# A decoder's gated-attention phase: the closing of each next batch's expert output is spread over three rounds, and the decay inputs move to later rounds

## The chip, the cores and the metric

One core of one Trainium2 chip runs the whole program. Times are microseconds of the device for one execution. The core has a matrix engine (TensorE, PE in the profile), a vector engine (VectorE, DVE), a scalar engine (ScalarE, ACT), GpSimd (POOL) and queues that issue transfers. They run their own instruction lists and meet only through semaphores. Lower is better.

## The reference, cut to what matters

The program is a decoder of two layers on `x` of shape (4, 512, 128): attention, cross attention and a mixture of experts, and then again gated linear attention, cross attention and a second mixture. After every block comes `x = layernorm(x + block(x))`. The change lies in the gated attention and in the end of the first mixture:

```python
q = silu(x @ Wq); k = silu(x @ Wk); v = x @ Wv      # 16 heads of 64
log_alpha = -softplus(x @ Wa + ba)
cum = cumsum(log_alpha, axis=1)
decay = exp(where(causal, cum[:, :, :, None] - cum[:, :, None, :], -inf))
o = ((q @ k.T) * decay) @ v
o = (o - mean) / sqrt(var + 1e-5) * gn_w + gn_b     # over sequence and head width
out = (o * sigmoid(x @ Wg)) @ Wo
...
# the mixture before it, whose result this phase starts from:
mixed = sum(topk_expert_outputs * topk_weights, axis=2)
x = layernorm(x + mixed)
```

## The kernel before, in words

The gated attention (`phase_d`) works on 4 batches of 8 head pairs. One pair is a **round**, g = 0 to 31 (four more empty the pipeline); b = g // 8 is the batch and s = g % 8 the place in it. Each engine has its own copy of the loop over g, and the order of the calls in it is written out by hand; an engine never takes a later instruction first.

In round g TensorE (lines 879 to 921) computes the state product of the pair before (`d_state(g - 1)`, L841), the query and key projections of the next pair (`d_proj(g + 1, 0)` and `(.., 1)`, L815 to L817, three matmuls each), the decays of the next pair (L796, L804, L806), the scores (L826), the gate projection of the pair before (`d_proj(g - 1, 2)`, again L815 to L817, after the second L806), a transpose (L832), and the output of pair g - 2 (`d_out`, L852 and L858). Then follows what only some rounds have: the group mean (`d_mean`, L868), a transpose of a closed batch (`turn_x`, L498), two value projections (`d_v`, L785), the alpha product (`d_alpha`, L759), the decay sums (`d_sums`, L767 to L771). A round is reckoned here from one first L841 to the next.

VectorE in round g: the state (`d_st`, L1762 and L1766), the two gated projections of the next pair (`d_silu`, L1728), the scores times decay (`d_at`, L1750), the decayed keys (`d_kd`, L1739), splits of weights and of x (L1494, L1495), statistics of pair g - 2 (`d_stats`, L1774 to L1780). After these comes what only some rounds have: `d_gated` (L1820, s = 1 and 5), `close_x`, `d_z` and `d_sp` (L1700 to L1708), `d_lsel` (L1369 to L1374 and a copy, L1715), `d_gate`. The next round begins with L1762 again.

`close_x(MOE[2], b)` ends the mixture of batch b: it waits for the gathered rows, adds them with their weights (8 instructions, L1674), takes statistics (L1307 to L1312), works out the reciprocal root in 11 small dependent instructions (L1317 to L1322) and writes the normalised x (L1332). Batch 0 is closed ahead of the phase, batches 1 to 3 inside the loop. Then `turn_x` and, on ScalarE, `keep_xT` (L959) lay the batch out transposed; `d_alpha`, `d_z`, ScalarE's `d_softplus` (L1175, L1176: an Exp and a Ln, each with a table load), `d_sp`, `d_sums`, `d_lsel` and ScalarE's `d_kdec` (L1182) follow on it. In rounds with s = 0 or 4 from g = 8 on, ScalarE also has `d_affine` (L1241), which in its list stands ahead of `d_softplus`.

Small products on TensorE share banks 6 and 7 in turn (`take_next`): each one waits until the reader of the product two places before it has read. So the gate projection of round g waits for VectorE's first L1728 of the same round, and a product that comes two places behind the decay sums waits for VectorE's `d_lsel`:

```python
            i = 6 + turn[0] % 2
            turn[0] += 1
            where[key] = bank[i]
            return take(pe, i, reader, value)
```

Of the kernel before, what the change touches and what calls it, by code (L numbers as in the profile page):

```python
# [35 lines left out]
NT = S // P  # L36
# [42 lines left out]
def decoder(nc, T):  # L79

    with ExitStack() as ctx:
# [13 lines left out]
        x_all = x_ext[:, :, 0:D]  # L95
        xT_all = sb("xT_all", [P, NB, S])
        yT = sb("yT", [P, S])
        res = sb("res", [P, NT, D])
# [136 lines left out]
        xh_D, xl_D = ([W0_low[:, 2048 + (2 * i + j) * S:2048 + (2 * i + j + 1) * S] for j in range(2)] for i in range(2))  # L235
        Q, K, V_, GATE = range(4)
        D_SPLITS = [(V_, 0), (Q, 0), (K, 0), (GATE, 0), (V_, 1), (Q, 1), (K, 1), (GATE, 1)]
        wqE, wkE, wvE, woE = (W0[:, i * 512:(i + 1) * 512] for i in range(4))

        ctxT = sb("ctxT", [P, NB * C])  # L240
# [223 lines left out]
        def _(pe):  # L464
# [405 lines left out]
            def phase_d():  # L870
                loaded(pe, "D", DMA_COUNT["D"])
                turn_x(PC)
                d_alpha(0)
                for t in range(NT):
                    d_v(0, 0, t)
                d_sums(0)
                d_proj(0, 0)
                d_proj(0, 1)
                d_decays(0)
                d_decay_to(0, 0)  # L880
                d_decay_to(0, 1)
                for g in range(32 + 4):
                    b, s = g // 8, g % 8
                    if 1 <= g <= 32:
                        d_state(g - 1)
                    if g + 1 < 32:
                        d_proj(g + 1, 0)
                        d_proj(g + 1, 1)
                        d_decays(g + 1)
                        d_decay_to(g + 1, 0)  # L890
                    if g < 32:
                        d_scores(g)
                    if g + 1 < 32:
                        d_decay_to(g + 1, 1)
                    if 1 <= g <= 32:
                        d_proj(g - 1, 2)
                    if g < 32:
                        d_kturn(g)
                    if 2 <= g < 34:
                        d_out(g - 2)  # L900
                    if s in (2, 6) and g >= 6:
                        d_mean((g - 6) // 4, 0)
                    if s in (3, 7) and g >= 7:
                        d_mean((g - 7) // 4, 1)
                    if g >= 16:
                        tail(PD + b - 2, s + 8)
                    if g in (1, 5, 9):
                        turn_x(PC + g // 4 + 1)
                    if g < 32:
                        if b:  # L910
                            tail(PD + b - 1, s)
                        if s in (2, 3):
                            d_v(b, 1, 2 * s - 4)
                            d_v(b, 1, 2 * s - 3)
                        if b + 1 < NB:
                            if s == 2:
                                d_alpha(b + 1)
                            if s == 4:
                                d_sums(b + 1)
                            if s in (6, 7):  # L920
                                d_v(b + 1, 0, 2 * s - 12)
                                d_v(b + 1, 0, 2 * s - 11)
# [9 lines left out]
        def _(act):  # L932
# [311 lines left out]
            def phase_d():  # L1244
# [9 lines left out]
                for g in range(32 + 4):  # L1254
# [10 lines left out]
                        d_affine((g - 8) // 4)  # L1265
                    if g >= 16:
                        tail(PD + b - 2, s + 8)
                    if g in (1, 5, 9):
                        keep_xT(PC + g // 4 + 1)
                    if g < 32:  # L1270
                        if b:
                            tail(PD + b - 1, s)
                        if s in (2, 3):
                            d_v(b, 1, 2 * s - 4)
                            d_v(b, 1, 2 * s - 3)
                        if b + 1 < NB:
                            if s == 2:
                                d_softplus(b + 1)
                            if s == 4:
                                d_kdec(b + 1)  # L1280
                            if s in (6, 7):
                                d_v(b + 1, 0, 2 * s - 12)
                                d_v(b + 1, 0, 2 * s - 11)
# [10 lines left out]
        def _(dve):  # L1294
# [370 lines left out]

            def close_x(m_, b):

                x = x_all[:, 4 * b:4 * b + 4, :]
                w = per_pair(wk, m_, b)
                dve.wait_ge(x_ready, m_["w0"] + b)  # L1670
                dve.wait_ge(sem(f"M_g{b}"), 32 + 16 * (m_["b0"] // NB))
                for k in range(m_["k"]):
# [5 lines left out]
                        dve.wait_ge(sem("M_cb"), m_["b0"] + b + 1)  # L1678
                    else:
                        link(i)  # L1680
                ln_stats(res)
                ln_apply(res, x).then_inc(x_ready, 1)


            def d_split_x(b):
# [137 lines left out]
            def phase_d():  # L1823
# [12 lines left out]
                for g in range(32 + 4):  # L1836
# [6 lines left out]
                    if g < 32:  # L1843
                        d_at(g)
                        d_kd(g)
                    for i in range(3 + 2 * g, min(5 + 2 * g, len(D_SPLITS))):
                        d_split_w(i)
                    if s == 5 and b + 1 < NB:
                        d_split_x(b + 1)
# [7 lines left out]
                        d_gated((g - 9) // 4, (0, 1, 2, 3))  # L1857
                    if g >= 16:
                        tail(PD + b - 2, s + 8)
                    if g in (0, 4, 8):  # L1860
                        close_x(MOE[2], g // 4 + 1)
                    if g < 32:
                        if b:
                            tail(PD + b - 1, s)
                        if b + 1 < NB:
                            if s == 2:
                                d_z(b + 1)
                                d_sp(b + 1)
                            if s == 4:
                                d_lsel(b + 1)  # L1870
                    if s in (3, 7) and g >= 7:
                        d_gate((g - 7) // 4)
# [190 lines left out]
```

## Time and profile before

| what | us |
|---|---|
| median of 3 runs | 1574.44 (1573.21 to 1575.3) |
| the profiled execution, its own time | 1578.1 |
| its span, first to last instruction | 1576.3 |
| TensorE matmuls busy | 1282.9 (81%) |
| VectorE busy | 849.2 (54%) |
| ScalarE busy | 834.8 (53%) |
| mean granted clock of TensorE | 0.921 of full |

The rows further down begin with the start and the duration in microseconds; a bracket at the end of a row is the time for which the engine stood idle before it, and what ended that. The granted clock is given in parts of 2.4 GHz; 0.5 is 1.2 GHz.

### The profile page before, as it was taken

To read this page: it belongs to the slowest core of one execution; us is meant where nothing else is said; L and a number is where in the kernel's file an instruction comes from. 1 tells how busy PE (TensorE), PEld (TensorE's weight loads), DVE (VectorE), ACT (ScalarE), POOL (GpSimd) and SP (SyncE) were. 2 spreads that over 40 slices of the span, in tenths; PEclk is the share of its full clock that TensorE was granted. 3 is DMA by queue.
4 is the path that set the end of the run, shared out by engine and by line. 5 is a ranking of instruction groups with operands and counts; after the bars stand their busy time and mean duration, and the time that the engine had idled before them with its cause. 6 is when DMAs were issued, how large, how long until landed. Compare 5 with 4: busy or idle time off the path is not lost.

```text
span 1576.3 us, 22676 instructions
## 1 busy us (share of the span) xinstructions
PE 1282.9 (81%) x6903; PEld 739.8 (47%) x6934; DVE 849.2 (54%) x2752; ACT 834.8 (53%) x1893; POOL 503.2 (32%) x473
## 2 busy tenths in 40 slices
PE   5999999999999987987645957788888886787552
PEld 2434444444344335544425955556565664444341
DVE  3544453364444336367552347777677876557535
ACT  4777677677767734544313634456465662344121
POOL 2555455445545512132453521001011010122242
PEclk9999999999999998998777979899999997898676
DMA  7235223220000000000026821000000000000053
GB/s 211 55 78 86 55 55 55 55 78 1 1 1 1 1 1 0 1 1 1 14 94 180 246 88 41 1 1 1 1 1 1 1 1 8 20 1 4 17 151 104
DMA packets 77701, 67.56 MB, mean 43 GB/s; under 512 B 5040, under 2 KB 68656, under 8 KB 77328
## 3 DMA queue, kind: packets, MB, share of 16 engines
q1 hardware_dynamic: 73488, 57.69, 15.2%
q0 software_dynamic: 3520, 7.27, 1.3%
q8 instruction: 60, 0.98, 0.3%
q10 hardware_dynamic: 576, 1.16, 0.2%
q14 instruction: 57, 0.47, 0.1%
HBM read 37.69 MB, written 28.41 MB: 42 GB/s over the span
## 4 chain that ended last, share of the span: by engine, by line
PE 63%; DVE 19%; issue 7%; ACT 6%; POOL 2%; DMA 2%; SPq 1%; DVEq 0%; POOLq 0%; ACTq 0%
PE bank L550 8%; PE bank L532 7%; PE bank L540 6%; PE bank L479 6%; PE bank L655 3%; PE bank L522 3%; PE bank L612 3%; PE bank L626 3%; PE bank L720 3%; PE bank L728 2%; PE bank L858 2%; DVE work L1381 2%; PE bank L641 2%; PE bank L852 1%; ACT work L996 1%
## 5 line engine op out<-in xcount | busy, mean ns | idle before, releaser
L1909 POOL TENSOR_TENSOR work<-work 128x512 f32<-128x512 f32 x256 | 266.1, 1040 | 272.5 <-DVE work L1389 272.5
L996 ACT ACTIVATE work<-bank,work 128x512 f32<-128x512 f32 x256 | 176.5, 689 | 117.4 <-DVE work L1381 117.3
L1381 DVE TENSOR_REDUCE work<-bank 128x1 f32<-128x512 f32 x256 | 176.4, 689 | 77.3 <-PE bank L532 77.0
L540 PEld LDWEIGHTS bank<-cst,work 128*128 128x128 f32 x1024 | 110.5, 140 | 164.4 <-issue 103.6
L540 PE MATMUL bank<-cst,work 128*128 128x128 f32 x1024 | 160.0, 283 | 6.6 <-ACT work L1004 6.0
L1389 DVE RECIPROCAL work<-work 128x1 f32<-128x1 f32 x256 | 41.9, 164 | 223.4 <-ACT work L996 223.0
L1004 ACT ACTIVATE work<-bank 128x512 f32<-128x512 f32 x256 | 152.6, 596 | 0.5 <-PE bank L540 0.5
L1991 POOL TENSOR_TENSOR work<-work 128x512 f32<-128x512 f32 x32 | 40.8, 1274 | 335.0 <-PE bank L858 294.3
L532 PE MATMUL bank<-work 64*128 64x512 f32 x512 | 144.5, 641 | 3.4 <-ACT work L996 3.4
L550 PE MATMUL bank<-work 128*64 128x512 f32 x512 | 137.4, 617 | 0.7 <-ACT work L1004 0.7
L1949 POOL TENSOR_TENSOR work<-work 128x1232 f32<-128x1232 f32 (+1 forms) x32 | 55.5, 1733 | 247.8 <-DVE work L1462 247.8
L1444 DVE TENSOR_REDUCE work<-bank 128x6 f32<-128x462 f32 (+1 forms) x80 | 38.9, 535 | 108.9 <-PE bank L626 108.9
L479 PE MATMUL bank<-OT,W 128*128 128x512 f32 x208 | 95.7, 604 | 0.7 <-DVE am L1568 0.7
L532 PEld LDWEIGHTS bank<-work 64*128 64x128 f32 x512 | 38.7, 184 | 97.0 <-issue 60.5
L1977 POOL DMA_INDIRECT yt<-work x62 | 59.3, 957 | 77.4 <-DVE work L1631 75.0
L1160 ACT ACTIVATE work<-bank,W 128x128 f32<-128x128 f32 x166 | 48.4, 369 | 63.0 <-PE bank L720 63.0
L1107 ACT ACTIVATE work<-bank 128x512 f32<-128x512 f32 x96 | 53.0, 595 | 54.0 <-PE bank L641 54.0
L641 PE MATMUL bank<-cst,work 128*128 128x128 f32 x384 | 59.2, 305 | 26.7 <-POOL work L1949 19.3
L815 PE MATMUL bank<-W_low 128*128 128x512 f32 x96 | 47.0, 490 | 38.3 <-DVE work L1728 17.2
L1208 ACT ACTIVATE work<-bank,work 128x128 f32<-128x128 f32 x256 | 72.4, 384 | 10.5 <-PE bank L806 10.5
L522 PE MATMUL bank<-W 128*128 128x512 f32 x128 | 69.2, 626 | 6.2 <-ACT work L984 3.8
L626 PE MATMUL bank<-work 128*128 128x154 f32 x384 | 61.2, 312 | 14.6 <-DVE work L1449 14.6
(246 smaller groups left out, 2457.2 us busy)
## 6 DMA issues: line engine op xcount, KB each, us to landing
xs<-gat SPq DMA_DIRECT2D x18, 1040.0 KB, 12.0
W<-in_w SPq DMA_DIRECT2D x30, 322.0 KB, 3.4
W<-in_w SPq DMA_DIRECT2D x23, 193.0 KB, 2.5
work<-xs SPq DMA_DIRECT2D x62, 65.0 KB, 3.5
gat<-yt SPq DMA_DIRECT2D x12, 256.0 KB, 3.0
work<-in_w SPq DMA_DIRECT2D x9, 322.0 KB, 3.4
W<-in_v SPq DMA_DIRECT2D x1, 2048.0 KB, 11.4
x_ext<-in_x SPq DMA_DIRECT2D x4, 256.0 KB, 8.4
```

What stands on the lines that cost most here:

```text
L479: m = mm(where["y", w][:, :], out_w(ph)[:, p * P:(p + 1) * P], o_slot(w, p), start=(p == 0), stop=(p == n - 1))
L522: mm(out[:, :], w[:, p * P:(p + 1) * P], xnT[b % 2], start=True, stop=True).then_inc(sem(ready), 1)
L532: m = mm(out[hh][:, :], qA[g % 2][HALF[hh], t * P:(t + 1) * P], kA[g % 2][HALF[hh], :], start=True, stop=True)
L540: m = nc.tensor.transpose(out[:, k * P:(k + 1) * P], pA[u % 5][:, k * P:(k + 1) * P], ident)
L550: m = mm(bank[5][hh * DH:(hh + 1) * DH, :], v3(vA[p // 4], NT)[:, k, (2 * (p % 4) + hh) * DH:(2 * (p % 4) + hh + 1) * DH], v3(ptA[(2 * g + ...
L626: m = mm(out[:, (p % 3) * 2 * C:(p % 3 + 1) * 2 * C], v3(qTB, NPAIR)[:, p, t * P:(t + 1) * P], kd, start=True, stop=True)
L641: m = nc.tensor.transpose(out[:, i * P:(i + 1) * P], pB[u % 3][:, h * C:h * C + P], ident)
L996: A(pA[u % 5], bank[u % 3][:, :], ACT.Exp, bias=nmax[:, u % 8:u % 8 + 1], accum_out=rsum[0][:, u % 8:u % 8 + 1]).then_inc(sem("a_e"), 1)
L1004: A(v3(ptA[h % 4], NT)[:, :, t * P:(t + 1) * P], v3(bank[3 + u % 2][:, :], NT), ACT.Copy)\
L1208: i = A(dmD[g % 2][:, (NT * hh + c) * P:(NT * hh + c + 1) * P], bank[1 - hh][:, c * P:(c + 1) * P], ACT.Exp, scale=-1.0, bias=lcD[b % 2][: ...
L1381: V.tensor_reduce(nmax[:, u % 8:u % 8 + 1], bank[u % 3][:, :], AX, ALU.max, negate=True)\
L1909: G.tensor_tensor(pA[u % 5], pA[u % 5], rsum[1][:, u % 8:u % 8 + 1].to_broadcast([P, S]), ALU.mult)\
```

## The change

1. `close_x` of batches 1 to 3 is cut into `close_step` parts 0, 1 and 2 (sum; statistics and root; normalise), one in each of the rounds g = 4k, 4k + 1 and 4k + 2. It stood whole in the rounds 0, 4 and 8. Batch 0 is still closed whole.
2. `turn_x` and `keep_xT` of these batches move from rounds 1, 5 and 9 to 3, 7 and 11.
3. `d_alpha`, `d_softplus`, `d_z` and `d_sp` of the next batch move from s = 2 to s = 4, `d_sums`, `d_kdec` and `d_lsel` from s = 4 to s = 5, in batches 0, 1 and 2.
4. The weight splits 3 to 7 stand in rounds 0, 1, 2, 2 and 3 in place of 0, 0, 1, 1 and 2.
5. At the start of the phase TensorE's `d_sums(0)` stands after two of the four value projections, not after all four.

```diff
+        SPLITS_AT = {0: (3,), 1: (4,), 2: (5, 6), 3: (7,)}
...
-                for t in range(NT):
+                for t in (0, 1):
                     d_v(0, 0, t)
                 d_sums(0)
+                for t in (2, 3):
+                    d_v(0, 0, t)
                 d_proj(0, 0)
...
-                    if g in (1, 5, 9):
+                    if g in (3, 7, 11):
                         turn_x(PC + g // 4 + 1)
...
-                            if s == 2:
+                            if s == 4:
                                 d_alpha(b + 1)
-                            if s == 4:
+                            if s == 5:
                                 d_sums(b + 1)
...
+            def close_step(m_, b, part):
+
+                if part == 0:
+                    close_sum(m_, b)
+                elif part == 1:
+                    ln_stats(res)
+                    ln_rstd()
+                elif part == 2:
+                    ln_apply(res, x_all[:, 4 * b:4 * b + 4, :], rstd=False).then_inc(x_ready, 1)
...
-                    for i in range(3 + 2 * g, min(5 + 2 * g, len(D_SPLITS))):
+                    for i in SPLITS_AT.get(g, ()):
                         d_split_w(i)
...
-                    if g in (0, 4, 8):
-                        close_x(MOE[2], g // 4 + 1)
+                    if g < 12:
+                        close_step(MOE[2], g // 4 + 1, g % 4)
```

ScalarE's and VectorE's loops have the same changes of s and of g as TensorE's.

**The closing of batch 1, on VectorE.** Before, rounds 0 and 1 meet here: `d_kd`, two splits, the whole closing (its first rows).

```order
L1739 TENSOR_TENSOR work<-bank,work 128x512
L1494 CAST W_low<-W 128x512
L1495 TENSOR_TENSOR W_low<-W,W_low 128x512
L1494 CAST W_low<-W 128x512
L1495 TENSOR_TENSOR W_low<-W,W_low 128x512
L1674 SCALAR_TENSOR_TENSOR res<-gat,wk,x_ext 128x128 x4
L1674 SCALAR_TENSOR_TENSOR res<-gat,wk,res 128x128 x4
L1307 BN_STATS bn<-res 128x6 x4
```

After, the same place, where the lines have moved down by 3 or 17 to 19 (L1739 is L1756, L1494 is L1497, L1674 is L1693, L1307 is L1310):

```order
L1756 TENSOR_TENSOR work<-bank,work 128x512
L1497 CAST W_low<-W 128x512
L1498 TENSOR_TENSOR W_low<-W,W_low 128x512
L1693 SCALAR_TENSOR_TENSOR res<-gat,wk,x_ext 128x128 x4
L1693 SCALAR_TENSOR_TENSOR res<-gat,wk,res 128x128 x4
L1779 TENSOR_SCALAR work<-bank 64x3x64 x2
L1783 SCALAR_TENSOR_TENSOR work<-work 64x64 x4
L1745 SCALAR_TENSOR_TENSOR work<-work,bank 128x512 x2
L1767 SCALAR_TENSOR_TENSOR work<-bank,work 128x512 x2
L1756 TENSOR_TENSOR work<-bank,work 128x512
L1497 CAST W_low<-W 128x512
L1498 TENSOR_TENSOR W_low<-W,W_low 128x512
```

The statistics now stand behind the VectorE work of one more pair and one split.

**The alpha of batch 3, on VectorE at the ends of rounds 20 and 21.** Before, from the splits of x in round 21 (the decay sums were read in round 20):

```order
L1739 TENSOR_TENSOR work<-bank,work 128x512
L1494 CAST W0_low<-xT_all 128x512
L1495 TENSOR_TENSOR W0_low<-xT_all,W0_low 128x512
L1774 BN_STATS work<-bank 128x6
L1776 BN_AGGR work<-work 128x2
L1779 COPY work<-work 128x1
L1780 COPY work<-work 128x1
L1820 SCALAR_TENSOR_TENSOR OT<-work,OT 128x512 x4
L1762 TENSOR_SCALAR work<-bank 64x3x64 x2
```

After, the same place (L1837 is the L1820 of before, L1372 to L1377 and L1732 are `d_lsel`):

```order
L1791 BN_STATS work<-bank 128x6
L1793 BN_AGGR work<-work 128x2
L1796 COPY work<-work 128x1
L1797 COPY work<-work 128x1
L1837 SCALAR_TENSOR_TENSOR OT<-work,OT 128x512 x4
L1372 CAST work<-bank 16x512
L1373 TENSOR_TENSOR work<-bank,work 16x512
L1375 CAST work<-work 16x512
L1376 COPY work<-work 16x512
L1377 TENSOR_TENSOR work<-work 16x512
L1732 COPY work<-bank 128x128
L1779 TENSOR_SCALAR work<-bank 64x3x64 x2
```

`d_lsel` now stands in the same round as `d_gated` and the split of x, behind both.

**The softplus of batch 3, on ScalarE at the end of round 20.** Before, round 20 has the affine and `d_kdec`:

```order
L1223 ACTIVATE work<-bank 128x512
L1232 ACTIVATE OT<-bank 128x512
L1241 ACTIVATE OT<-OT,work 128x512 x4
L1182 ACTIVATE work<-work 128x64
L1218 ACTIVATE work<-bank 128x512 x2
L1198 ACTIVATE work<-bank 128x512
```

After (L1244 is the affine, L1178 and L1179 the softplus with its table load, L1221 the next tanh with its own):

```order
L1226 ACTIVATE work<-bank 128x512
L1235 ACTIVATE OT<-bank 128x512
L1244 ACTIVATE OT<-OT,work 128x512 x4
L1178 ACTIVATE work<-work 128x64
L1179 ACT_TABLE_LOAD
L1179 ACTIVATE work<-work 128x64
L1221 ACT_TABLE_LOAD
L1221 ACTIVATE work<-bank 128x512 x2
```

The softplus and its two table loads now stand behind the affine and ahead of the next pair's tanh.

## Rows read from the trace of the kernel before

**Rows 1.** The page: busy time and share of the span.

```profile
PE 1282.9 (81%) x6903; PEld 739.8 (47%) x6934; DVE 849.2 (54%) x2752; ACT 834.8 (53%) x1893; POOL 503.2 (32%) x473
```

**Rows 2.** Waits of TensorE, 935 to 1335 us: total, times, longest.

```profile
PE bank L815 <- DVE work L1728: 17.2, 9, 7.0
```

**Rows 3.** Timeline of TensorE at the closings of batches 2 and 3.

```profile
1012.10 0.77 PE L815 MATMUL bank<-W_low 128*128 128x512 f32 x1 [7.57 <-DVE work L1370]
...
1061.68 0.76 PE L815 MATMUL bank<-W_low 128*128 128x512 f32 x1 [4.78 <-DVE work L1728]
...
1066.93 0.66 PE L498 MATMUL bank<-cst,x_ext 128*128 128x128 f32 x4
...
1091.68 0.83 PE L841 MATMUL bank<-work 128*128 128x128 f32 x6
```

**Rows 4.** Stretches: busy us of PE, PEld, DVE, ACT, POOL; granted clock; DMA.

```profile
1060.00:1066.00 6.00, 4.32 (x19) 3.72 (x21) 3.94 (x8) 0.00 (x0) 0.00 (x0) 0.50 0.00 0
1106.00:1114.00 8.00, 6.73 (x61) 5.11 (x57) 7.53 (x16) 3.73 (x12) 1.28 (x1) 1.00 0.00 0
```

**Rows 5.** Timeline of VectorE, the closing of batch 3 in round 8.

```profile
1051.79 1.15 DVE L1674 SCALAR_TENSOR_TENSOR res<-gat,wk,x_ext 128x128 f32<-128x128 f32 x4
...
1054.14 0.87 DVE L1307 BATCH_NORM_STATS2 bn<-res 128x6 f32<-128x128 f32 x4
...
1057.85 1.12 DVE L1332 TENSOR_SCALAR x_ext<-res,mv,lnv 128x128 f32<-128x128 f32 x4
1058.88 0.71 DVE L1762 TENSOR_SCALAR work<-bank 64x192 f32<-64x192 f32 x2
```

**Rows 6.** Timelines at the phase's start: TensorE, VectorE, ScalarE.

```profile
942.78 0.77 PE L785 MATMUL bank<-W_low 128*128 128x512 f32 x1
...
948.84 0.29 DVE L1715 COPY work<-bank 128x128 f32<-128x128 f32 x1
...
945.44 1.28 ACT L1182 ACT_TABLE_LOAD   x1
```

**Rows 7.** Timeline of TensorE, rounds 19 to 23.

```profile
1172.50 0.91 PE L841 MATMUL bank<-work 128*128 128x128 f32 x6
...
1178.20 0.39 PE L804 MATMUL bank<-work,sel 128*128 128x512 bf16 x1 [1.43 <-ACT work L1198]
...
1191.56 1.05 PE L767 MATMUL bank<-cst,work 128*16 128x128 f32 x8
...
1193.04 0.89 PE L841 MATMUL bank<-work 128*128 128x128 f32 x6
1194.42 0.47 PE L815 MATMUL bank<-W_low 128*128 128x512 f32 x1 [0.50 <-DVE work L1370]
...
1196.21 0.47 PE L815 MATMUL bank<-W_low 128*128 128x512 f32 x1 [0.85 <-DVE work L1715]
...
1199.28 0.58 PE L815 MATMUL bank<-W_low 128*128 128x512 f32 x1
...
1202.39 0.94 PE L841 MATMUL bank<-work 128*128 128x128 f32 x6
...
1209.00 0.47 PE L815 MATMUL bank<-W_low 128*128 128x512 f32 x1 [0.26 <-DVE work L1728]
...
1212.00 0.39 PE L868 MATMUL bank<-work,cst 128*128 128x4 f32 x2
...
1221.47 0.83 PE L841 MATMUL bank<-work 128*128 128x128 f32 x6
```

**Rows 8.** Timelines of ScalarE and VectorE, rounds 18, 20 and 21.

```profile
1173.43 0.26 ACT L1175 ACTIVATE work<-work 128x64 f32<-128x64 f32 x1 [0.94 <-DVE work L1703]
...
1192.95 2.92 ACT L1241 ACTIVATE OT<-OT,work 128x512 f32<-128x512 f32 x4
...
1175.43 0.72 DVE L1762 TENSOR_SCALAR work<-bank 64x192 f32<-64x192 f32 x2
...
1203.59 2.69 DVE L1820 SCALAR_TENSOR_TENSOR OT<-work,OT 128x512 f32<-128x512 f32 x4
```

More of the change, by code:

```diff
@@ L1267, in phase_d @@
                         tail(PD + b - 2, s + 8)
-                    if g in (1, 5, 9):
+                    if g in (3, 7, 11):
                         keep_xT(PC + g // 4 + 1)
@@ L1276, in phase_d @@
                         if b + 1 < NB:
-                            if s == 2:
+                            if s == 4:
                                 d_softplus(b + 1)
-                            if s == 4:
+                            if s == 5:
                                 d_kdec(b + 1)
@@ L1666, in close_x, with close_sum @@
             def close_x(m_, b):
+                close_sum(m_, b)
+                ln_stats(res)
+                ln_apply(res, x_all[:, 4 * b:4 * b + 4, :]).then_inc(x_ready, 1)
+            def close_step(m_, b, part):
+                if part == 0:
+                    close_sum(m_, b)
+                elif part == 1:
+                    ln_stats(res)
+                    ln_rstd()
+                elif part == 2:
+                    ln_apply(res, x_all[:, 4 * b:4 * b + 4, :], rstd=False).then_inc(x_ready, 1)
+            def close_sum(m_, b):
                 x = x_all[:, 4 * b:4 * b + 4, :]
@@ L1680, in close_x @@
                         link(i)
-                ln_stats(res)
-                ln_apply(res, x).then_inc(x_ready, 1)
             def d_split_x(b):
@@ L1865, in phase_d @@
                         if b + 1 < NB:
-                            if s == 2:
+                            if s == 4:
                                 d_z(b + 1)
                                 d_sp(b + 1)
-                            if s == 4:
+                            if s == 5:
                                 d_lsel(b + 1)
```

## The prediction

> **What bounds the kernel now.** The page first: matmuls are busy 81% of the span, VectorE and ScalarE just over half [rows 1]. So TensorE sets the time wherever nobody keeps it waiting, and an edit that issues the same instructions in another order is worth what it takes from, or adds to, TensorE's waits. The waits of TensorE over the phase come next: the largest group is the projection L815 waiting for VectorE's L1728, 17.2 us in 9 waits, the longest 7.0 [rows 2]. The timeline says where. After the closing of batch 2 the first projection waited 7.57 us, after that of batch 3 the gate projection 4.78 [rows 3]; the 7.0 of [rows 2] is the closing of batch 1. The closing is one block on VectorE: 2.35 us of sum, 3.71 of statistics and root, 1.03 of normalising, 7.09 together (1051.79 to 1058.88) [rows 5]. VectorE cannot start the next pair's L1762 before it, and the gate projection starts 2.80 us after that L1762 (1058.88 to 1061.68) [rows 3, 5].
>
> A long wait costs twice. In 1060 to 1066 the granted clock is 0.50, the lower of its two levels, and it is 1.00 in 1106 to 1114, a stretch with short waits only [rows 4]. From gate projection to the end of the output product took 5.25 us at the low level (1061.68 to 1066.93) and 3.00 at full (1209.00 to 1212.00) [rows 3, 7]: 2.25 us for each wait after which the clock is down. What TensorE did before it fell was nothing, for 4.8 to 7.6 us.
>
> The Trainium skill, "TensorE: Matmul & The Clock Gate", section "HAM oscillation — how this bites in real kernels", takes the penalty as half of the time spent at the low level. For the six microseconds of [rows 4] that is 3.0 where the rows give 2.25; six falls would cost 18 by the page and 13.5 by the rows.
>
> **Where the change gains: rounds 0 to 11.** I followed the rounds one by one with the durations of before. VectorE's own chain from one L1762 to the next is some 7.2 us in a round with nothing extra, TensorE's 7.5; of extra work at the round's end about 1.8 us is free. The three closings cost TensorE 7.0, 7.57 and 4.78 us of idle time, another 1.5 us where ScalarE was late in the third, and three stretches of low clock, some 6.8 together: 27.7. The alpha of batches 1 and 2 in rounds 2 and 10 cost some 5 more (1.4 each at L804, as in 1178.20 [rows 7], and waits for banks). All of it goes, about 32.
>
> What comes in its place, at full clock, with the parts of [rows 5]:
> - Start: `d_sums(0)` can start at 942.78, when bank 6 is read, some 2.1 us earlier than it did. But it takes both banks, and the third and fourth value projections then wait for `d_lsel` and its copy (L1715). So the fourth ends 0.7 us after the copy, ScalarE reads it, and only then comes the table load, 1.28 us, that before ran at 945.44 under cover of `d_lsel` [rows 6]. The copy is 1.7 us earlier (948.84 to 947.1), the tanh behind it 1.0 later, the next exponential 0.6. Cost +0.6; the bounds are -1.9 (all of the earlier sums) and +1.3 (the whole load).
> - Round 0 ends with a split and the sum, 3.4 us: stall 1.5. Round 1 with a split and the statistics, 4.8: stall 3.0. Round 2 with two splits ahead of the statistics of the pair, which ScalarE's reads wait for: 1.4.
> - Round 4: sum 2.35, then `d_z`, softplus, `d_sp`: stall 4.2 in round 5, in two pieces, since the second projection also waits for `d_z`.
> - Round 5: split of x, statistics 3.71, then `d_lsel` with its 2.9 to the copy, all before round 6: 4.35 us idle, one projection, 1.0 more.
> - Round 8: sum; ScalarE's affine hides most: 0.3. Round 9: `d_gated` 2.6 and statistics 3.71 meet: 1.5 for a bank and 4.4 in one piece. The third parts, in rounds 2, 6 and 10, are 1.03 us and hidden by the value projections (1.4) behind the output product.
>
> Together some 22. Counted from round start to round start, round 12 begins at 1080.5 at full clock and 1091.68 before [rows 3]: **-11.2 us**, of which 0.8 is alpha not yet done.
>
> **Where it loses: rounds 12 to 15 and 19 to 23.** Nothing is closed here; only the alpha has moved, next to other work. Batch 3, by [rows 7, 8]:
> - Round 19 starts 0.8 earlier (no alpha), 1171.7, and has no wait of 1.43. Rounds 19 and 20 took 20.54 us (1172.50 to 1193.04); less the 1.5 of waiting, less 1.48 of sums (1191.56 to 1193.04), plus 0.8 of alpha: round 21 starts at 1190.1, and the output product ahead of it ends at 1189.3.
> - ScalarE starts the affine 1.39 us after that end (1191.56 to 1192.95) and is free 2.8 later: 1193.5. Then softplus, first Exp to the next L1762, 2.00 (1173.43 to 1175.43): 1195.5. L804 comes 2.77 after (1175.43 to 1178.20), at 1198.3, the gate projection 0.25 later. TensorE is through with its scores 4.3 us into a round (1178.20 less 1.43, from 1172.50), at 1194.4. **A new wait of 3.9 us.** Before, the affine stood over `d_lsel`, both hidden from each other; now VectorE waits for the Ln behind it.
> - The output product ends at 1201.5, the sums at 1203.0. VectorE has statistics 1.1, `d_gated` 2.6 (L1820), `d_lsel` to the copy 2.9, 0.4 to the projection: 1208.8 for the second, 1207.0 for the first (they are 1.79 apart at 1194.42 and 1196.21). **A new wait of 3.2 and then 1.1 us**, for 0.50 and 0.85 before.
> - Then as before: 3.07 to the gate projection (1196.21 to 1199.28), 12.47 to round 23 (1209.00 to 1221.47): it starts at 1224.3, for 1221.47. **+2.8 us.**
>
> Batch 2 has the same in rounds 12 to 15, but the 2.3 us that its round 10 gained is already in the -11.2: **+4.9**. At full clock the change so gives -11.2 + 4.9 + 2.8 = **-3.5 us**.
>
> **The clock.** The new waits are 3.0 (round 2), 2.5 (5), 4.35 and 1.0 (6), 4.4 (10), 3.9 (13), 3.2 and 1.1 (14), 3.9 (21), 3.2 and 1.1 (22). Before, three long waits lowered the clock in this phase and none of the short ones, up to 1.58 us, did. A wait of 3.9 lies between, nearer to the 4.78 that did; I count all of 3.9 us and more as falls (4 of them), the pair 3.2 + 1.1 as falls too, since they are one projection apart (2), and half for each of rounds 2 and 5 at about 2 us. With 2.25 us each this is 6 x 2.25 + 1.5 = 15, less some 1.3 where VectorE is last anyway: **+13.7**. Bounds: nothing, and 8 x 2.25 = 18.
>
> **Sum.** -3.5 + 13.7 = +10.2. The walk is made on the profiled execution (1578.1, 1576.3 of it span; 3.7 above the median), which would go to about 1588. On the median: 1574.4 + 10 = **1584 us**. Every long wait that the closing left is cut, and the number of waits long enough to lower the clock goes from three to some six.
>
> **Rivals.**
> 1. *The clock holds.* New waits of 3 to 4.4 us are shorter than any of the three that lowered it here. Then the time is 1574.4 - 3.5 = **1571**. Against: 3.9 to 4.4 is only a little under 4.78. Chance 0.15. It decides the sign: with two falls (4.5 us) the change is already no gain.
> 2. *The spreading works as it reads.* VectorE is idle almost half of the span [rows 1] and might take parts of 2.35, 3.71 and 1.03 us in its gaps, with the alpha as cheap as before. Then the 27.7 us of the closings go and the new waits stay at some 10: about **1560**. What speaks against it is that only 1.8 us per round is free and that in rounds 5 and 9 two pieces meet. Chance 0.07.
> 3. *Some falls only.* Only two or three of the six waits lower the clock, or they are shorter than worked out: +1 to +4, **1577**. Chance 0.20.
> 4. *My sum*, six or more falls: 1578 to 1591, **1584**, chance 0.58.
>
> **How the numbers follow.** What a measurement of this kernel can tell from no change is about 0.2%, 3.1 us: the three runs of before span 2.1. Faster by more than that is rival 2 and half of rival 1 with a little of 3: 0.17. Within it: the other half of 1, most of 3 and the edge of 4: 0.19. Slower 0.64. The range reaches from the full-clock case, 1570, to all eight falls with the start at its bound, 1591; less than 2 in 10 is outside, rival 2 above all. The likeliest case alone has 1578 to 1591.
>
> **What would show each step.** After the change, no wait of TensorE over 5 us in the phase; at the start, the tanh behind `d_kdec` about 1 us later, ScalarE's table load after the fourth value read. In rounds 13 and 21 a wait of L804 for ScalarE's L1198 (L805 and L1201 then) of about 4 us, with VectorE waiting some 4 us for the Ln; in rounds 14 and 22 a wait of the first projection for `d_lsel`, 3 us, and one of 1 behind it. Stretches at 0.50 after these, six in place of three. If the stretch of rounds 12 to 23 is not longer than before, my softplus step is wrong; if it is longer by under 8 us, the clock was oversized. If the first twelve rounds gain less than 5 us, the closings' parts cost more than I took.

## The result and the profile after

| | before | after |
|---|---|---|
| median | 1573.83 us, 4 runs (1573.15 to 1575.3) | 1586.56 us, 4 runs (1584.61 to 1587.15) |
| ratio to before | | 1.0077 (95% interval 1.006 to 1.0095) |
| profiled execution, its own time and span | 1578.1, 1576.3 | 1587.15, 1585.3 |
| mean granted clock | 0.921 | 0.916 |

The change makes the kernel 0.8% slower. The page of after has the same work as [rows 1], with 4.9 us more of matmul time on the same 6903 matmuls:

```profile
PE 1287.8 (81%) x6903; PEld 744.9 (47%) x6934; DVE 850.7 (54%) x2752; ACT 835.3 (53%) x1893; POOL 503.4 (32%) x473
```

**Where the time went.** The rounds of both traces were laid beside each other by their first state product, counted from the start of the phase (its L498 or L499; 935.52 in the span of before, 933.17 in that of after). The difference, after less before, in us:

| start of round | 1 | 2 | 6 | 7 | 10 | 12 | 14 | 15 | 18 | 21 | 22 | 23 | 26 | 32 |
|---|---|---|---|---|---|---|---|---|---|---|---|---|---|---|
| later by | 1.6 | -5.1 | -7.7 | -0.9 | -7.6 | -4.0 | 2.3 | 3.4 | 3.4 | 0.4 | 8.2 | 8.6 | 10.1 | 10.2 |

The phase starts 2.35 earlier in its span and what follows it takes 1.2 longer, so the span grows by 9.0. Nothing of the edit stands ahead of the phase, and in the eleven traces of this document it starts anywhere from 930.5 to 935.7, so the 2.35 is no merit of the change. The medians differ by 12.7, more than the spans, because the traced execution of before was 4.3 above its kernel's median and that of after 0.6 above. From one trace to another a step of the table over the same instructions repeats within some 0.1 us where the clock does the same in both, and moves by about 1.6 with a short fall of it. The table is read by its steps. The closings gain in rounds 1, 5 and 9, as meant. Much of it is lost at once, 6.8 in round 6 and 4.5 in round 10. From round 12 on nothing is gained that lasts: from round 12 to 15 it loses 7.4 us, from 18 to 23 5.2 and from 25 to 26 1.6, together 14.2.

The waits of TensorE over the phase (total, times, longest) show what took the place of [rows 2]. The largest group is no longer for VectorE's projections but for ScalarE:

```profile
PE bank L805 <- ACT work L1201: 16.7, 8, 3.8
PE bank L816 <- DVE work L1745: 11.2, 9, 4.0
PE bank L816 <- DVE work L1373: 6.3, 3, 4.1
PE bank L816 <- ACT work L1226: 5.7, 4, 1.6
...
PE bank L771 <- ACT work L1226: 3.5, 2, 1.8
```

On TensorE's timeline the place of [rows 7] now has these waits in two rounds (L842 is the state product, L805 the decays, L771 the second decay-sum product, L816 the projections):

```profile
1191.13 0.91 PE L842 MATMUL bank<-work 128*128 128x128 f32 x6
...
1199.18 0.61 PE L805 MATMUL bank<-work,sel 128*128 128x512 bf16 x1 [3.78 <-ACT work L1201]
...
1207.71 0.43 PE L771 MATMUL bank<-work,cst 128*128 128x64 f32 x2 [1.76 <-ACT work L1226]
1208.20 0.89 PE L842 MATMUL bank<-work 128*128 128x128 f32 x6
1210.23 0.47 PE L816 MATMUL bank<-W_low 128*128 128x512 f32 x1 [1.14 <-DVE work L1373]
...
1212.01 0.47 PE L816 MATMUL bank<-W_low 128*128 128x512 f32 x1 [0.85 <-DVE work L1732]
```

The first wait is explained by ScalarE's timeline of the same stretch. The affine ends at 1194.5, and only then come the Exp, the Ln and the tanh of the next pair (L1221). There are two table loads of 1.28 us, one ahead of the Ln and one ahead of the tanh; the Exp has none of its own, in before neither (it starts at 1173.43, the Ln's load at 1173.70), although the description of the kernel before gives it one. L805 waits for L1201 behind that tanh:

```profile
1191.61 2.92 ACT L1244 ACTIVATE OT<-OT,work 128x512 f32<-128x512 f32 x4
1194.43 0.24 ACT L1178 ACTIVATE work<-work 128x64 f32<-128x64 f32 x1
1194.69 1.28 ACT L1179 ACT_TABLE_LOAD   x1
1195.98 0.26 ACT L1179 ACTIVATE work<-work 128x64 f32<-128x64 f32 x1
1196.26 1.28 ACT L1221 ACT_TABLE_LOAD   x1
...
1198.52 0.60 ACT L1201 ACTIVATE work<-bank 128x512 f32<-128x512 f32 x1
...
1207.06 0.60 ACT L1226 ACTIVATE work<-bank 128x512 f32<-128x512 f32 x1 [5.67 <-DVE OT L1837]
```

VectorE stands 4.03 us for that Ln with the whole next pair behind it, and later runs `d_gated` (L1837) and `d_lsel` (L1372 to L1732) in one piece:

```profile
1196.27 0.23 DVE L1725 SCALAR_TENSOR_TENSOR work<-work 128x64 f32<-128x64 f32 x1 [4.03 <-ACT work L1179]
...
1206.10 2.67 DVE L1837 SCALAR_TENSOR_TENSOR OT<-work,OT 128x512 f32<-128x512 f32 x4
1208.69 0.67 DVE L1372 CAST work<-bank 16x512 bf16<-16x512 f32 x1
```

The closings' parts are felt most in rounds 5, 6 and 10, where they meet the softplus, `d_lsel` or `d_gated`:

```profile
1006.24 0.61 PE L805 MATMUL bank<-work,sel 128*128 128x512 bf16 x1 [2.24 <-ACT work L1201]
...
1017.66 0.77 PE L816 MATMUL bank<-W_low 128*128 128x512 f32 x1 [4.07 <-DVE work L1373]
...
1067.79 0.76 PE L816 MATMUL bank<-W_low 128*128 128x512 f32 x1 [3.96 <-DVE work L1745]
```

And the clock. Of these stretches of after (length; busy us of PE, PEld, DVE, ACT, POOL; granted clock; DMA) each holds one fall, in the start and in rounds 2, 5, 6, 10, 13, 14, 21 and 25; before has three falls among its rounds (1, 5 and 9), the last of them in [rows 4]:

```profile
943.00:947.00 4.00, 2.64 (x7) 1.94 (x8) 2.03 (x5) 0.65 (x2) 0.00 (x0) 0.73 0.00 0
964.00:968.00 4.00, 2.98 (x12) 2.55 (x11) 3.79 (x16) 0.37 (x1) 0.01 (x1) 0.66 0.53 178
1004.00:1008.00 4.00, 1.76 (x6) 1.20 (x6) 3.80 (x9) 3.89 (x11) 0.00 (x0) 0.78 0.01 2
...
1018.00:1022.00 4.00, 3.50 (x9) 1.55 (x9) 3.81 (x11) 1.64 (x4) 0.00 (x0) 0.50 0.02 4
...
1069.00:1073.00 4.00, 4.00 (x31) 3.46 (x30) 1.66 (x3) 0.60 (x1) 0.39 (x1) 0.73 0.00 0
...
1102.00:1106.00 4.00, 4.00 (x19) 3.25 (x19) 2.49 (x5) 1.89 (x7) 0.00 (x0) 0.59 0.00 0
1111.00:1116.00 5.00, 3.59 (x8) 1.90 (x10) 4.71 (x13) 1.22 (x3) 0.00 (x0) 0.66 0.00 0
1199.00:1203.00 4.00, 3.82 (x14) 3.06 (x14) 2.49 (x6) 2.29 (x9) 0.00 (x0) 0.50 0.00 0
1254.00:1257.00 3.00, 2.31 (x11) 2.16 (x12) 2.78 (x5) 1.10 (x5) 0.00 (x0) 0.74 0.00 0
```

A value between 0.5 and 1 says that the low level held for a part of the stretch. There are nine falls in place of three, seven of them shorter than that of [rows 4]. Round 22 has the waits of round 14 and no fall:

```profile
1205.00:1225.00 20.00, 16.09 (x92) 9.90 (x93) 13.30 (x33) 5.57 (x15) 2.53 (x2) 1.00 0.00 1
```

### The profile page after: what moved, and what is told of

It is laid out like the page before. It is cut to its first block, busy times and chain, and to the rows that moved or that the text cites. A ratio compares the mean times of both kernels' runs of the same rounds, so it can differ in the third digit from the quotient of the medians.

```text
span 1585.3 us, 22679 instructions
## 1 busy us (share of the span) xinstructions
PE 1287.8 (81%) x6903; PEld 744.9 (47%) x6934; DVE 850.7 (54%) x2752; ACT 835.3 (53%) x1893; POOL 503.4 (32%) x473
## 4 chain that ended last, share of the span: by engine, by line
PE 62%; DVE 19%; issue 7%; ACT 7%; POOL 2%; SPq 1%; DMA 1%; POOLq 0%; DVEq 0%; ACTq 0%
PE bank L551 8%; PE bank L533 7%; PE bank L541 6%; PE bank L480 6%; PE bank L656 3%; PE bank L523 3%; PE bank L613 3%; PE bank L721 3%; PE bank L627 3%; PE bank L729 2%; PE bank L859 2%; DVE work L1384 2%; PE bank L642 2%; PE bank L853 1%; ACT work L999 1%
## 5 line engine op out<-in xcount | busy, mean ns | idle before, releaser
L1211 ACT ACTIVATE work<-bank,work 128x128 f32<-128x128 f32 x256 | 72.7, 382 | 10.2 <-PE bank L807 9.6
L816 PE MATMUL bank<-W_low 128*128 128x512 f32 x96 | 49.2, 513 | 28.1 <-DVE work L1745 11.2
## 6 DMA issues: line engine op xcount, KB each, us to landing
xs<-gat SPq DMA_DIRECT2D x18, 1040.0 KB, 11.8
```

What stands on the lines that cost most here:

```text
L1211: i = A(dmD[g % 2][:, (NT * hh + c) * P:(NT * hh + c + 1) * P], bank[1 - hh][:, c * P:(c + 1) * P], ACT.Exp, scale=-1.0, bias=lcD[b % 2][: ...
```

## The experiments

Theory A, that of the prediction: the closings' parts gain a few us, the moved alpha loses more, a good part of it through the clock. Its rival B: the parts themselves are the loss, and where the alpha stands hardly matters. A second question is how the loss divides into ScalarE's collision (round 13 and 21), VectorE's (14 and 22) and the clock. The ratios are to before in the same set of runs, with 95% intervals. Times in the phase are counted from its start, as in the table above.

### 1. The alpha of batches 2 and 3 back in its old rounds

The changed kernel, with the rounds of the alpha and its sums as before from batch 1's on; the alpha of batch 1 stays where the change put it, since batch 1 is closed later. The same edit stands in ScalarE's and VectorE's loops.

```diff
-                            if s == 4:
+                            if s == (4 if b == 0 else 2):
                                 d_alpha(b + 1)
-                            if s == 5:
+                            if s == (5 if b == 0 else 4):
                                 d_sums(b + 1)
```

> The changed kernel, but for batches 2 and 3 (decided in rounds 8 and up) alpha and softplus are back at s = 2 and the decay sums back at s = 4; the first batch's stay at 4 and 5, since its x is closed later. My theory (the loss is made in rounds 12 to 15 and 19 to 23, where softplus stands behind the affine and the decay sums behind the gated product): both losses go, about 7 and 5 us, and round 10 gets some 3 us of stall back: 1575 us, with the same start of round 6 as in the changed kernel. Rival (the three parts of the closing are the loss): within 3 us of the changed kernel's 1586.6.

Measured: 1575.1 us, ratio 0.9997 (0.9985 to 1.0008). Round 12 starts 3.8 earlier than before, round 15 still 3.9 earlier, and 2.3 remain at the end, after a fall of the clock in round 17 (1.6). Against the trace of after that is 10.2 + 2.3 = 12.5 us, and the ratios say the same (0.9997 for 1.0077, 12.6 us). So the whole loss belongs to the alpha of batches 2 and 3, and B falls. Whether the closings in parts with the new start gain anything is not shown: 2.3 us between two single traces, but a ratio whose interval holds 1. With the start's 1.0012 (experiment 3) taken off, the parts alone would gain some 2.4 us, which is an estimate; no run has them alone.

### 2. The alpha alone

The kernel before, with `d_alpha` and its followers moved as in the change in the batches 1 and 2 (b > 0), and nothing else.

```diff
-                            if s == 2:
+                            if s == (2 if b == 0 else 4):
                                 d_alpha(b + 1)
-                            if s == 4:
+                            if s == (4 if b == 0 else 5):
                                 d_sums(b + 1)
```

> The kernel before, with alpha and softplus of batches 2 and 3 alone moved to s = 4 and the sums to s = 5; closings whole, start as before. My theory: 5 us lost per batch, 1573.8 + 10 = 1584 us, with waits of TensorE for ScalarE of 3.8 us in rounds 13 and 21. Rival (alpha is free to move): 1574 us.

Measured: 1590.89 us, ratio 1.0089 (1.0076 to 1.0102), 14 us over before where 10 were expected. Its waits show the same collision without any part of a closing:

```profile
PE bank L804 <- ACT work L1198: 15.6, 8, 3.8
```

From the start of round 12 to that of 15 it loses 6.8 us, from 21 to 23 8.0, and in rounds 17 and 25 1.6 each, where the clock fell. Less what rounds 10 and 11 (2.4) and 18 to 20 (2.9) gain, the two batches cost 4.4 and 5.1, as counted. What had not been counted are the 3.2 of falls in rounds that the edit doesn't touch.

### 3. The start alone

The kernel before, with `d_sums(0)` after two of the four value projections (the last piece of the change's diff).

> The kernel before with only the first decay sums moved between the second and the third value projection. My theory: both banks are taken, the table load is uncovered, and the clock may fall: +0.6 to +1.6 us, 1575 us. Rival (sums that are ready earlier help): -1.9 us, 1572 us.

Measured: 1578.89 us, ratio 1.0012 (1.0003 to 1.0021). Round 1 starts 1.63 later and all later ones by the same. The start costs 1.6 us in the traces, 1.9 by the ratio, and is not paid back.

### 4. The first new wait filled

The changed kernel, with 16 idle products in rounds 13 and 21, where TensorE waits for ScalarE. Their result is never read and the real work is the same. If the low clock comes from TensorE's doing nothing, it must stay away.

```diff
                         d_scores(g)
+                    if g in (13, 21):
+                        pe.wait_ge(sem("d_o"), g - 2)
+                        for _ in range(16):
+                            mm(bank[5][:, :], ident_b[:, :], mask[:, :], start=True, stop=True)
```

> The changed kernel, with 16 idle products of constants (128x512, bf16, into a bank that is overwritten next) behind the scores of rounds 13 and 21, which keep TensorE at work during the waits of 3.8 us. The result is unchanged. My theory (each fall of the clock costs about 2.25 us): the stretches at 0.50 behind these two waits go and the time falls by 3 to 4.5 us, to about 1583. Rival (VectorE and ScalarE are last there, so TensorE's clock costs nothing): 1586.6 us, unchanged.

Measured: 1589.08 us, ratio 1.0077 (1.0064 to 1.009): no gain over the change. The stretches say why:

```profile
1098.00:1106.00 8.00, 7.75 (x58) 4.86 (x59) 5.49 (x14) 7.08 (x16) 0.00 (x0) 1.00 0.00 0
1112.00:1116.00 4.00, 3.64 (x8) 1.73 (x10) 3.78 (x12) 1.47 (x4) 0.00 (x0) 0.50 0.00 0
1196.00:1205.00 9.00, 8.65 (x67) 5.44 (x68) 6.25 (x15) 7.33 (x17) 0.00 (x0) 1.00 0.00 0
1210.00:1214.00 4.00, 3.76 (x8) 1.82 (x10) 3.77 (x11) 1.23 (x3) 0.00 (x0) 0.50 0.00 0
```

Where the fillers ran, the clock stayed at full, and round 14 starts level with before in place of 2.3 later. One round on, the waits for the sums' readers brought the clock down instead, and by round 23 the kernel is 8.3 later than before, against 8.6 in after. Part of this is a fall in round 17 (0.57 in 1158 to 1162), which cost 1.6 and which after does not have. My expectation overlooked that the second waits suffice by themselves, in round 22 too, where after had kept the full clock.

### 5. Both new waits filled

The same, with 8 idle products ahead of the second decay-sum product of batches 2 and 3 and 5 behind the state product of rounds 14 and 22.

```diff
                 m.then_inc(sem("d_LT"), 1)
+                if b >= 2:
+                    pe.wait_ge(sem("d_dm"), 16 * b - 2)
+                    for _ in range(8):
+                        mm(bank[0][:, :], ident_b[:, :], mask[:, :], start=True, stop=True)
                 out = take_next(pe, ("d_lc", b), sem("d_lcs"), b + 1)
...
                         d_state(g - 1)
+                    if g in (14, 22):
+                        for _ in range(5):
+                            mm(bank[0][:, :], ident_b[:, :], mask[:, :], start=True, stop=True)
```

> As the run with 16 idle products in rounds 13 and 21, and besides 8 such products ahead of the second decay-sum product of these rounds and 5 behind the state product of rounds 14 and 22, so that TensorE works through most of both waits. The result is unchanged. My theory (in the run before, the falls only moved from the first wait to the second): with both covered no stretch at 0.50 stays in rounds 13, 14, 21 and 22, and each batch gains 2 to 4 us over the changed kernel: 1581 us on the scale of 1586.6. Rival (the clock costs nothing there, others are last): 1586.6.

Measured: 1579.96 us, ratio 1.0027 (1.0015 to 1.0039), for 1.0077 of the change. The clock stays at full through both places:

```profile
1098.00:1106.00 8.00, 7.60 (x55) 4.84 (x54) 7.74 (x17) 4.49 (x13) 1.26 (x1) 1.00 0.00 0
1190.00:1215.00 25.00, 23.70 (x159) 14.61 (x158) 19.42 (x47) 12.13 (x30) 2.53 (x2) 1.00 0.00 1
```

With the clock up, rounds 12 to 15 lose 5.1 us and rounds 18 to 23 2.8, and no round after them anything. In after the same stretches lose 7.4 and 5.2, and round 25 1.6. So of after's 14.2 us behind round 12 the clock makes 6.3 and the collisions make 7.9. This division rests on one trace of each kernel, this one the fastest of twelve executions (1577.3), and whatever the fillers themselves cost is in the 7.9. Another 2.0 us by which this kernel is ahead at round 12 are no merit of the fillers: ahead of them the instructions are those of after. Most of it is round 5, where the same wait of 2.24 us was followed by a fall in after (0.78 in 1004 to 1008, above) and by none here:

```profile
1004.00:1008.00 4.00, 2.47 (x17) 2.03 (x19) 3.83 (x9) 4.00 (x12) 0.00 (x0) 1.00 0.00 2
```

### 6. The softplus ahead of the affine

The changed kernel, with ScalarE's `d_softplus` called before `d_affine` in rounds with s = 4. Then the two swap who waits, if VectorE's `d_sp` is the one that keeps the next pair.

```diff
+                    if s == 4 and b + 1 < NB:
+                        d_softplus(b + 1)
                     if s in (0, 4) and g >= 8:
                         d_affine((g - 8) // 4)
...
-                            if s == 4:
-                                d_softplus(b + 1)
```

> The changed kernel with ScalarE's softplus ahead of the affine in rounds with s = 4. Theory A (what ends TensorE's wait of 3.8 us is ScalarE's whole list, affine and softplus and table loads, whatever their order): no gain, 1586 to 1589 us, the wait of TensorE for L1201's counterpart at 3.8 us or a little more. Theory B (VectorE waiting for the Ln is what counts): the Ln comes 2.2 us earlier, twice, 1582 us.

Measured: 1588.54 us, ratio 1.0081 (1.0067 to 1.0095), as the change. The wait of the decays even grew, from 3.78:

```profile
1199.60 0.61 PE L805 MATMUL bank<-work,sel 128*128 128x512 bf16 x1 [4.48 <-ACT work L1201]
```

In its trace the phase takes 3.7 longer than in after; it has falls in rounds 17 and 22 that after does not have (and none at the start or in 25), and the ratios do not tell the two kernels apart. So putting the softplus first gains nothing; my reading, which no run separates further, is that both stand between two pairs, and the decays wait for the tanh behind both.

### 7. The sums alone

The kernel before, with only `d_sums`, `d_kdec` and `d_lsel` of batches 2 and 3 at s = 5. The alpha and the softplus stay at s = 2, so ScalarE's collision in rounds 13 and 21 can't arise.

```diff
-                            if s == 4:
+                            if s == (4 if b == 0 else 5):
                                 d_sums(b + 1)
```

> The kernel before, with only the decay sums (and what reads them) of batches 2 and 3 moved from s = 4 to s = 5; alpha and softplus stay at s = 2, closings whole. If the collision with the gated product is the larger part of what alpha_only lost (14 us over before): 1573.8 + 8 to 10, about 1583. If it is the affine and softplus: 1573.8 + 2 to 4, about 1577. I take the second to be likelier by my sum (waits of 3.2 and 1.1 us in place of 1.4 and 1.5, with one fall of the clock per batch).

Measured: 1585.87 us, ratio 1.0059 (1.0046 to 1.0073), against some 1577 expected. The step that I had thought the lesser half makes most of the loss: 9.3 us of 14.0 by the ratios, 9.8 of 11.8 in the phase of the two traces. The alpha and the softplus add the rest, 4.7 or 1.9; it is little for waits of 3.8, since moving them also ends the waits that they caused in their old rounds. Rounds 13 and 14 cost 4.4 us and 21 and 22 4.9, and falls of the clock in rounds 17 and 25 2.9 and 1.6. These last 4.5, in rounds that the edit doesn't touch, are the larger part of what the expectation missed; experiment 2 has 3.2 of the same. TensorE's timeline in round 21 shows what I had not counted:

```profile
1207.04 0.43 PE L770 MATMUL bank<-work,cst 128*128 128x64 f32 x2 [1.76 <-ACT work L1223]
...
1209.56 0.77 PE L815 MATMUL bank<-W_low 128*128 128x512 f32 x1 [0.55 <-DVE work L1370]
1211.35 0.77 PE L815 MATMUL bank<-W_low 128*128 128x512 f32 x1 [0.17 <-DVE work L1715]
```

The second decay-sum product takes the bank of the gate projection. Its reader is ScalarE's tanh of the gate, L1223, and that one waits for VectorE's `d_gated`, which reads what it will overwrite (5.67 us in after, at 1207.06 above). At s = 4 there is no `d_gated`; at s = 5 the sums stand behind it.

### 8. Batch 3 closed whole in round 14

From the change: the alpha as in experiment 1, the start as before, batches 1 and 2 closed in thirds, and batch 3 closed whole at the end of round 14, whose end on TensorE is long (before it takes 19 us). Its `turn_x` and `keep_xT` move to round 15.

```diff
-                    if g < 12:
+                    if g < 8:
                         close_step(MOE[2], g // 4 + 1, g % 4)
+                    if g == 14:
+                        close_x(MOE[2], 3)
...
-                    if g in (3, 7, 11):
-                        turn_x(PC + g // 4 + 1)
+                    if g in (3, 7, 15):
+                        turn_x(PC + (1, 2, 0, 3)[g // 4])
```

> A version of my own: closings of batches 1 and 2 in thirds, alpha of batches 2 and 3 at s = 2 and sums at s = 4, start as before, and batch 3 closed whole in round 14, where VectorE waits 8.27 us for TensorE's output projection, with its transpose in round 15. Theory: the start's 1.6 us and the third closing's 4 to 5 us go, against the run with alpha back (0.9997 of before): ratio about 0.9955, 1567 us. Rival (a closing costs its 7 us wherever VectorE has it): ratio 0.999 or more.

Measured: 1568.51 us, ratio 0.9947 (0.9934 to 0.996). Rounds 9 and 10 take 22.0 us for 29.7 before. Round 14 takes 19.1, as before: VectorE has done with the whole closing and still waits for TensorE:

```profile
1113.64 1.14 DVE L1691 SCALAR_TENSOR_TENSOR res<-gat,wk,x_ext 128x128 f32<-128x128 f32 x4
...
1119.70 1.12 DVE L1333 TENSOR_SCALAR x_ext<-res,mv,lnv 128x128 f32<-128x128 f32 x4
1121.99 0.72 DVE L1777 TENSOR_SCALAR work<-bank 64x192 f32<-64x192 f32 x2 [1.17 <-PE bank L842]
```

The rounds 5, 6 and 7, though, take 42.6 us for 39.2 before (40.6 in experiment 1): closing batch 2 in thirds in rounds 4 to 6, with batch 1's alpha in rounds 4 and 5, costs more there than closing it whole had. Some 2 of these 3.4 us are one fall of the clock in round 5, which experiment 1 does not have with the same instructions and the same wait (2.25 and 2.24). First experiment 1, then this kernel:

```profile
1008.00:1012.00 4.00, 3.67 (x34) 3.03 (x35) 3.87 (x8) 2.82 (x10) 0.05 (x1) 1.00 0.00 0
1008.00:1012.00 4.00, 3.69 (x15) 3.04 (x15) 3.09 (x7) 2.80 (x10) 0.00 (x0) 0.63 0.00 0
```

### 9. Batch 2's parts in rounds 6, 8 and 9 as well

```diff
-                    if g < 8:
-                        close_step(MOE[2], g // 4 + 1, g % 4)
+                    if g < 4:
+                        close_step(MOE[2], 1, g)
+                    if g in (6, 8, 9):
+                        close_step(MOE[2], 2, (6, 8, 9).index(g))
```

The turn of batch 2 moves to round 10.

> The version with batch 3 closed in round 14, and batch 2's three parts moved from rounds 4, 5 and 6 to rounds 6, 8 and 9, with its transpose in round 10: away from the softplus of round 4 and the decay sums of round 5, into rounds where VectorE's time is short or ScalarE's affine makes TensorE wait anyway. Theory (a part costs only where it meets other work behind the same output product): rounds 5 to 8, 42.6 us in the run with batch 3 in round 14, fall to 32 to 34, and round 9 loses about 1: 8 us less, 0.9947 goes to about 0.990, 1560 us. Rival (the parts cost their time in any round): within 2 us of 1568.5.

Measured: 1565.04 us, ratio 0.9926 (0.9913 to 0.9939): faster than both kernels, 0.3% short of what was expected. Rounds 5 to 7 take 32.5 us. Rounds 9 and 10 take 27.3 for 22.0 in experiment 8, where I had expected 1 us more: the statistics stand where batch 2's alpha is, and TensorE waits five times, each time briefly. The clock also fell there (0.57 in 1046 to 1050).

```profile
1044.27 0.39 PE L805 MATMUL bank<-work,sel 128*128 128x512 bf16 x1 [1.54 <-ACT work L1199]
1046.27 0.47 PE L816 MATMUL bank<-W_low 128*128 128x512 f32 x1 [1.40 <-DVE work L1743]
...
1053.75 0.47 PE L816 MATMUL bank<-W_low 128*128 128x512 f32 x1 [1.28 <-ACT work L1224]
...
1058.48 0.47 PE L816 MATMUL bank<-W_low 128*128 128x512 f32 x1 [1.28 <-DVE work L1743]
...
1063.10 0.47 PE L786 MATMUL bank<-W_low 128*128 128x512 f32 x1 [0.75 <-DVE work L1805]
```

## Why the prediction was right, and where its terms were off

The forecast was 1584 us, slower, at a chance of 0.64; 1586.56 came, inside the likeliest case's 1578 to 1591. Inside the phase the trace of after is 10.2 us longer, for +10.2 in the sum. That the sum fits so closely is partly luck, as its terms show, and the medians differ by 12.7 rather than 10.2.

- **The closings' gain, rounds 0 to 11.** -11.2 at full clock and three falls' worth of clock (6.8) made -4.5 at round 12; -4.0 came. Experiment 5, with one fall less, has -6.0. Experiment 1 ends 2.3 us ahead of before in its trace, but its ratio of 0.9997 does not show that anything of it lasts. The waits came nearly as worked out: for a stall of 1.5 behind round 0, 1.19; for 3.0 behind round 1, 1.01 and 2.54 in experiment 5 (1.01 and 0.96 in after, where the clock had fallen ahead of the second); for 4.2 in round 5, 1.51 and 2.24; for 4.35 and 4.4 in rounds 6 and 10, 4.07 and 3.96. My test for this step, a gain of under 5 us by round 12 as a sign that the parts cost more than I took, was badly put: it was met by the 4.0, but my own sum had -4.5 there with the clock.
- **The start.** +0.6 was forecast, 1.6 came (experiment 3 too). The mechanism is as told: the fourth value is read, and only then comes the table load, at 947.56. In experiment 4, which has the same start, the clock did not fall there (1.00 in 945 to 949 for 0.73 in 943 to 947 of after), and round 1 came 0.77 later than before. Experiment 6, with no fall there either, has 0.48; experiments 1, 3 and 5, with one, have 1.6 to 1.7. The term missing was the clock: the waits of 0.99 and 0.85 after a stretch of little work were not counted as such that may lower it.
- **The softplus, rounds 13 and 21.** A wait of 3.9 of L804 for ScalarE was forecast, 3.81 and 3.78 came, with VectorE 4.03 behind the Ln for "some 4".
- **The sums, rounds 14 and 22.** A wait of 3.2 and one of 1.1 were forecast. The trace has 1.76, 1.14 and 0.85 (0.17 in round 14): nearly the same total, in other pieces. The step "`d_sums` costs 1.48 and then the projection waits for `d_lsel`" left out that the second product itself waits for the gate's tanh behind `d_gated`. Experiment 7 shows it alone.
- **Rounds 12 to 15 and 18 to 23 at full clock.** +4.9 and +2.8 were forecast; with the clock kept up (experiment 5) they are +5.1 and +2.8. This is the best part of the prediction, though the terms listed for VectorE in round 21 (1.1, 2.6, 2.9 and 0.4 from 1201.5) end at 1208.5 and not at 1208.8, which would give +2.5.
- **No wait over 5 us** held for the rounds: the longest is 4.07. The one of 5.6 for ScalarE's L1235, at the phase's end, is in before too.
- **The clock.** 2.25 us per fall was too much for these. The pairs of rounds 13 and 14 and of 21 and 22 were counted as four falls; three came (13, 14 and 21), and they cost 4.7 together, 1.6 each. A short fall in round 17 or 25 costs 1.6 too, and the longer one of experiment 7 in round 17 2.9, so the price goes with the length, and most of these are shorter than that of [rows 4]. From round 12 to 23 the kernel loses 12.6 where the terms give some 15. The whole wait was also taken for what lowers the clock. In before it was down well before the waits ended: 0.84 in 1059 to 1060, while the wait of 4.78 ran from 1056.90 to 1061.68. So a wait of 3.9 was not clearly short of those that lowered it. (The sum has a slip as well: half of each of rounds 2 and 5 at about 2 us makes 2.0, and 1.5 was added.) On the other side there are more falls: nine in place of the six to seven counted. One of them, in round 25, follows waits of 1.52 and 0.99, which the trace of before has as well, at 1.00 throughout. Too few falls at too high a price made about the right sum for the whole phase.
- **The rivals.** The clock did not hold (1), the alpha was not as cheap as before (2), and there were more falls, not fewer (3). With the fillers of experiment 5 the full-clock case can be seen: 1.0027, and not the 0.998 that rival 1 gave, since falls in the first rounds remain and fillers have to be issued.

What stays open is why a wait of a given length is followed by a fall in one kernel and not in another. The wait of 2.24 in round 5 did it in after and not in experiment 5. The pair of 1.5 and 1.0 stands in rounds 17 and 25 of all eleven traces, and the clock fell there in 11 of the 22 cases. The Trainium skill, "TensorE: Matmul & The Clock Gate", section "What's actually happening", says that the window in which TensorE's activity is watched runs freely and does not start with the kernel, so that the cold start of one and the same kernel differs from run to run. The two traces of round 5 are in keeping with that (0.78 and 1.00), but no run here shows the window itself, and no kernel was traced twice. It was not tried to shift such a wait by small steps.

## What to carry to other kernels

A block that is moved to a later round must be read against everything that stands in the new round, on every engine: here the softplus met ScalarE's affine (a wait of 3.8), and the decay sum, which cost more on balance, took a bank whose reader waits for VectorE's long `d_gated`. Cutting a block into thirds gained little where the parts met other work (experiment 1, 0.9997, of it 0.0012 the cost of the start), and more where they were moved away from it (experiment 9, 0.9926 for 0.9947); one place where the engine that sets the time has a long stretch of its own (round 14) hid the whole 7 us block at no cost. And a wait on TensorE has to be priced twice, itself and the clock behind it, with the second price uncertain by its own size.

## What the runs showed of the hardware

- The granted clock also fell at waits well below the shortest that lowered it before (4.78 us): at 3.8, 2.24, and a pair of 1.5 and 1.0. Equal waits in equal instructions had 0.78 in one kernel and 1.00 in another, and the pair had a fall in round 17 of seven of the eleven traces and in round 25 of four.
- Rounds 17 and 25 take 10.9 us at full clock and 12.5 with one short fall in them (0.86 over the round). Experiment 7 had a longer one in round 17 (0.75), and the round took 13.8.
- Idle products in the waits kept the granted clock at 1.00 (experiments 4 and 5). Covering one of two neighbouring waits moved the fall to the next one and gained nothing, covering both gained 0.5%. About 2 us of the 8 that the traces show for this come from rounds ahead of the fillers.
